# Cross attention with value rows per head and 64x64 products instead of context products

## The reference

```
x = layernorm(x + ttt_attention(x))          # chunked linear attention, 16 heads of 16
x = layernorm(x + cross_attention(x, ctx))   # this part changes
x = layernorm(x + ffn_int8_like(x))          # w_gate_up (1408, 256), w_down (256, 704)

# cross_attention: 16 heads of 128
q = rmsnorm(x @ Wq) * gq;  k = rmsnorm(ctx @ Wk) * gk;  v = ctx @ Wv
P = softmax(q k^T / sqrt(128))               # per batch and head, 64 x 64
out = concat_heads(P v) @ Wo                 # (16, 64, 256)
```

## Time and profile before

| | us |
|---|---|
| median of 3 runs | 442.09 (441.3 to 442.74) |
| the profiled execution | 441.95 |
| its span | 440.1 |
| PE busy | 362.4 (82%) |
| PEld busy | 212.4 (48%) |
| DVE busy | 266.0 (60%) |
| ACT busy | 218.0 (50%) |
| POOL busy | 120.9 (27%) |

### The profile page before, as it was taken

The page is one execution under the profiler, slowest core; times in us unless marked ns, Lnnn a source line. Parts: engine busy times, 40 slices in busy tenths (PEclk is TensorE's granted clock), DMA queues, the critical chain, the costliest instruction groups (busy, mean ns, idle before and its releaser), DMA issues.

```text
span 440.1 us, 10666 instructions
## 1 busy us (share of the span) xinstructions
PE 362.4 (82%) x4506; PEld 212.4 (48%) x4506; DVE 266.0 (60%) x494; ACT 218.0 (50%) x584; POOL 120.9 (27%) x132
## 2 busy tenths in 40 slices
PE   3999979779977735596799999999999999996942
PEld 2445844435433212343465665755757557473621
DVE  1579945499996886504243384673946728367564
ACT  3035954545533333063646757468475584753320
POOL 3042891022040041103033332343223432233001
PEclk9999969988968969589899999999999999998975
DMA  8990000000323001901010010100100100000000
GB/s 260 240 365 11 1 4 5 3 4 3 81 75 101 2 0 35 211 7 48 0 41 11 1 48 12 44 6 13 49 12 25 25 14 0 12 3 0 12 0 25
DMA packets 17630, 19.93 MB, mean 45 GB/s; under 512 B 3360, under 2 KB 15024, under 8 KB 17328
## 3 DMA queue, kind: packets, MB, share of 16 engines
q1 hardware_dynamic: 17552, 19.24, 16.0%
q10 hardware_dynamic: 32, 0.02, 0.0%
HBM read 18.07 MB, written 1.18 MB: 44 GB/s over the span
## 4 chain that ended last, share of the span: by engine, by line
PE 50%; DVE 19%; ACT 13%; POOL 8%; issue 7%; DMA 1%; SPq 1%; POOLq 0%; DVEq 0%; ACTq 0%
PE ps L626 9%; PE ps L535 7%; PE ps L672 5%; PE ps L446 5%; PE ps L525 4%; PE ps L680 3%; PE ps L640 3%; PE ps L572 3%; POOL pr L1525 3%; POOL pr L1527 3%; PE ps L554 3%; PE ps L649 2%; DVE pr L1382 2%; DVE pr L1379 2%; DVE mx L1381 2%
## 5 line engine op out<-in xcount | busy, mean ns | idle before, releaser
L626 PE MATMUL ps<-xwq,x1t 128*128 128x512 f32 x128 | 65.0, 638 | 0.9 <-ACT x1t L997 0.9
L680 PE MATMUL ps<-mvo,cxp 128*128 128x256 f32 x256 | 58.4, 382 | 0.1
L680 PEld LDWEIGHTS ps<-mvo,cxp 128*128 128x128 f32 x256 | 47.6, 190 | 6.7 <-issue 0.4
L535 PE MATMUL ps<-ctxt,xwk 128*128 128x512 f32 x64 | 39.0, 716 | 2.4 <-issue 2.2
L975 ACT ACTIVATE qjunk<-ps 128x128 f32<-128x128 f32 x128 | 33.5, 280 | 9.9 <-PE ps L626 9.7
L896 ACT ACTIVATE ksq<-ps 128x512 f32<-128x512 f32 x32 | 19.0, 594 | 38.3 <-PE ps L525 28.2
L626 PEld LDWEIGHTS ps<-xwq,x1t 128*128 128x128 f32 x128 | 24.0, 202 | 27.5 <-issue 24.7
L985 ACT ACTIVATE qt<-ps 128x512 f32<-128x512 f32 x32 | 19.2, 601 | 23.4 <-PE ps L640 23.3
L525 PE MATMUL ps<-ksq,onehot 128*32 128x512 f32 x64 | 21.8, 680 | 9.2 <-ACT ksq L896 9.1
L672 PE MATMUL ps<-pt,ctx 64*128 64x512 f32 x64 | 28.0, 657 | 0.2 <-ACT cxp L1006 0.2
L975 ACT ACTIVATION_READ_ACCUMULATOR qjunk<-ps 128x1 f32 x128 | 27.1, 212 | 0.0
(11 more groups left out here) (212 smaller groups left out, 736.5 us busy)
## 6 DMA issues: line engine op xcount, KB each, us to landing
rkb<-kscale SPq DMA_DIRECT2D x16, 256.0 KB, 4.0
xn<-in_x_dram SPq DMA_DIRECT2D x4, 512.0 KB, 5.4
ctx<-in_ctx_dram SPq DMA_DIRECT2D x4, 512.0 KB, 8.7
xwo<-in_L_xattn_Wo_dram SPq DMA_DIRECT2D x1, 2048.0 KB, 14.2
xwq<-in_L_xattn_Wq_dram SPq DMA_DIRECT2D x4, 512.0 KB, 5.4
w1n<-in_L_ffn_w_gate_up_dram SPq DMA_DIRECT2D x1, 1408.0 KB, 8.9
xwv<-in_L_xattn_Wv_dram SPq DMA_DIRECT2D x1, 1024.0 KB, 11.0
xwk<-in_L_xattn_Wk_dram SPq DMA_DIRECT2D x1, 1024.0 KB, 16.5
```

The costliest lines, as they stand in the source:

```text
L535: mm(bank(6 + n % 2), xwk[:, h * XD:(h + 1) * XD], ctxt[:, half * BANK:(half + 1) * BANK], start=True, stop=True)\
L626: last = mm(bank(n % 2), x1t[:, (i % 2) * D + k * P:(i % 2) * D + (k + 1) * P], xwq[qn][:, k * BANK:(k + 1) * BANK], start=k == 0, stop=k ...
L680: last = mm(bank(6 + turn_of[("y", i, 0)] % 2, D), cxp[:, h * P:(h + 1) * P], mvo[:, h * D:(h + 1) * D], start=h == 0, stop=h == XH - 1)
```

## The change

The context products and their tile `cxp` go. `value_rows` computes, per tile, ctx (128 rows, both batches) times `mvo` in 8 products of 512 columns, with the same stationary operand (`ctxt`, the transposed context that the keys use); ACT copies them into two tiles `z0` and `z1`, which lie over the context and over Wk of the cross attention. `attention_out` then multiplies, per head and batch, a 64 x 64 block of transposed P by 64 rows of these, 256 columns. The two batches of a head use the upper and the lower 64 partitions of both SBUF and PSUM. `p_transpose` becomes 32 products of 64 x 64 blocks with the identity, so that batch 0 comes out in the upper and batch 1 in the lower half. The value rows of tile 0 are computed in iterations -1 and 0, those of tile i-1 (i from 2) in iteration i. The second load of the context goes. `krow1` moves to another place, and ACT waits for its DMAs before it writes there. `sg` and `gs` of the FFN become one tile.

```diff
+        vrows = [place("z0", XH * D // 2, over="ctx2"), place("z1", XH * D // 2, over="xwk")]
...
+        krow1 = place("krow1", BANK, over="qjunk")
...
-            for half in range(2):
-                load(ctx2[half * T:(half + 1) * T, :].rearrange("p (b c) -> p b c", c=CD), ctx_in.rearrange("b s c -> s b c"), "ctx")
...
                 for n in range(2):
                     bk = open_tp("pt", i, n)
-                    for t in range(4):
-                        col = (i % 2) * XH * T + (n * 4 + t) * P
-                        last = nc.tensor.transpose(bank(bk, P, t * P), pr[:, col:col + P], ident[:, :])
+                    for t in range(8):
+                        for b2 in range(2):
+                            part = slice(b2 * T, (b2 + 1) * T)
+                            col = (i % 2) * XH * T + (n * 8 + t) * T
+                            last = mm(ps[part, bk * BANK + t * T:bk * BANK + (t + 1) * T], pr[part, col:col + T], ident[part, part],
+                                      start=True, stop=True)
...
+            def value_rows(i, n):
+                bk = open_turn("z", i, n)
+                turn_done(mm(bank(bk), ctxt[:, i * P:(i + 1) * P], mvo[:, n * BANK:(n + 1) * BANK], start=True, stop=True))
...
             def attention_out(i, heads):
                 for h in heads:
                     if h == 0:
-                        wait(turn_emptied("cp", i, 3))
+                        pe.wait_ge(sem("tp_evac"), tp_of[("pt", i, 1)] + 1)
+                        wait(turn_emptied("z", i, 3))
                         open_turn("y", i)
-                    last = mm(bank(6 + turn_of[("y", i, 0)] % 2, D), cxp[:, h * P:(h + 1) * P], mvo[:, h * D:(h + 1) * D],
-                              start=h == 0, stop=h == XH - 1)
+                    if h == XH // 2:
+                        wait(turn_emptied("z", i, 7))
+                    at = (6 + turn_of[("y", i, 0)] % 2) * BANK
+                    for b2 in range(2):
+                        part = slice(b2 * T, (b2 + 1) * T)
+                        zh = vrows[h // 8][part, (h % 8) * D:(h % 8 + 1) * D]
+                        last = mm(ps[part, at:at + D], pt[part, h * T:(h + 1) * T], zh, start=h == 0, stop=h == XH - 1)
...
+                if n == 0:
+                    act.wait_ge(sem("k_rows_out"), 64)
...
+            def value_rows_out(i, n):
+                bk = turn("z", i, n)
                 if n == 0 and i >= 1:
                     act.wait_ge(sem("turn_done"), turn_of[("y", i - 1, 0)] + 1)
-                o = cxp[:, :].rearrange("p (h r q) -> p r h q", r=2, q=P)[:, odd, :, b2 * T:(b2 + 1) * T]
-                freed(A(o, bank(bk).rearrange("p (h q) -> p h q", q=T), ACT.Copy))
+                freed(A(vrows[n // 4][:, (n % 4) * BANK:(n % 4 + 1) * BANK], bank(bk), ACT.Copy))
```

More of the change, by code:

```diff
@@ L127, in decoder_block @@
         ctxt = place("ctxt", B * T)
-        krow1 = place("krow1", BANK, over="ctxt")
         pR = place("pR", NCH * CW)
@@ L192, in decoder_block @@
         qjunk = place("qjunk", BANK)
+        krow1 = place("krow1", BANK, over="qjunk")
         assert cursor[0] <= at_of["xwk"]
-        cxp = place("cxp", XH * P)
-        gs = place("gs", FF)
-        assert cursor[0] <= at_of["pR"]
+        vrows = [place("z0", XH * D // 2, over="ctx2"), place("z1", XH * D // 2, over="xwk")]
         xwq = []
@@ L204, in decoder_block @@
         cursor[0] = at_of["sgR"] + KT * BANK
-        sg = place("sg", FF)
+        gs = place("gs", FF)
         hq = place("hq", FF // 2, BF16)
@@ L292, in decoder_block @@
         for i, cur, prev, last2, last3, nxt, nxt2 in pipeline():
+            later = i - 1 if i >= 2 and prev else None
+            first = 0 if i == 0 else None
+            if later is not None:
+                turns += [("z", later, 0, "act"), ("z", later, 1, "act")]
             turns += [("down", i - 3, 0, "dve")] * last3
-            turns += [("cp", i - 1, n, "act") for n in range(2)] * prev
+            if first is not None:
+                turns += [("z", 0, 4, "act"), ("z", 0, 5, "act")]
+            if later is not None:
+                turns += [("z", later, 2, "act"), ("z", later, 3, "act")]
             turns += [("wo", i + 2, 0, "dve")] * nxt2
-            turns += [("cp", i - 1, n, "act") for n in range(2, 4)] * prev
-            turns += [("gu", i - 2, n, "dve") for n in range(4)] * last2
+            if i == -1:
+                turns += [("z", 0, n, "act") for n in range(4)]
+            if first is not None:
+                turns += [("z", 0, 6, "act"), ("z", 0, 7, "act")]
+            if later is not None:
+                turns += [("z", later, 4, "act"), ("z", later, 5, "act")]
+            turns += [("gu", i - 2, n, "dve") for n in range(2)] * last2
+            if later is not None:
+                turns += [("z", later, 6, "act")]
+            turns += [("gu", i - 2, n, "dve") for n in range(2, 4)] * last2
+            if later is not None:
+                turns += [("z", later, 7, "act")]
             turns += [("y", i - 1, 0, "dve")] * prev
@@ L738, in _ @@
             for i, cur, prev, last2, last3, nxt, nxt2 in pipeline():
+                later = i >= 2 and prev
                 if cur:
                     q_quarter(i, 0)
+                if later:
+                    value_rows(i - 1, 0)
                 if last3:
@@ L744, in _ @@
                     q_quarter(i, 1)
+                if later:
+                    value_rows(i - 1, 1)
                 if prev:
@@ L748, in _ @@
                     ffn_down(i - 3)
+                if i == 0:
+                    value_rows(0, 4)
                 if cur:
@@ L751, in _ @@
                     q_transpose(i, 0)
-                if prev:
-                    context_sum(i - 1, 0)
-                    context_sum(i - 1, 1)
+                if i == 0:
+                    value_rows(0, 5)
+                if later:
+                    value_rows(i - 1, 2)
                 if cur:
                     q_quarter(i, 3)
+                if later:
+                    value_rows(i - 1, 3)
+                if cur:
                     q_transpose(i, 1)
@@ L759, in _ @@
                     ttt_out(i + 2)
-                if prev:
-                    context_sum(i - 1, 2)
+                if i == -1:
+                    for n in range(4):
+                        value_rows(0, n)
+                if i == 0:
+                    value_rows(0, 6)
+                if later:
+                    value_rows(i - 1, 4)
                 if cur:
                     q_transpose(i, 2)
+                if i == 0:
+                    value_rows(0, 7)
                 if last2:
                     x_transpose_q(i - 2)
-                if prev:
-                    context_sum(i - 1, 3)
+                if later:
+                    value_rows(i - 1, 5)
                 if last2:
                     gate_up(i - 2, range(0, 2))
+                if later:
+                    value_rows(i - 1, 6)
                 if cur:
@@ L773, in _ @@
                     gate_up(i - 2, range(2, 4))
+                if later:
+                    value_rows(i - 1, 7)
                 if cur:
@@ L1015, in silus @@
                     act.wait_ge(*turn_emptied("gu", i, 2 * n))
-                    A(sg[:, n * FP:(n + 1) * FP], gs[:, n * FP:(n + 1) * FP], ACT.Silu, scale=sx[:, 8 * (i % 3):8 * (i % 3) + 1])\
+                    A(gs[:, n * FP:(n + 1) * FP], gs[:, n * FP:(n + 1) * FP], ACT.Silu, scale=sx[:, 8 * (i % 3):8 * (i % 3) + 1])\
                         .then_inc(sem("sg_ready"), 1)
             for i, cur, prev, last2, last3, nxt, nxt2 in pipeline():
+                later = i >= 2 and prev
                 if cur:
                     q_quarter(i, 0)
+                if later:
+                    value_rows_out(i - 1, 0)
                 if last3:
@@ L1025, in _ @@
                     q_quarter(i, 1)
+                if later:
+                    value_rows_out(i - 1, 1)
                 if prev:
@@ L1028, in _ @@
                     tp_out("pt", i - 1, 1)
+                if i == 0:
+                    value_rows_out(0, 4)
                 if cur:
@@ L1031, in _ @@
                     q_quarter(i, 2)
-                if prev:
-                    context_out(i - 1, 0)
-                    context_out(i - 1, 1)
+                if i == 0:
+                    value_rows_out(0, 5)
+                if later:
+                    value_rows_out(i - 1, 2)
+                    value_rows_out(i - 1, 3)
                 if cur:
@@ L1037, in _ @@
                     q_quarter(i, 3)
-                if prev:
-                    context_out(i - 1, 2)
+                if i == -1:
+                    for n in range(4):
+                        value_rows_out(0, n)
+                if i == 0:
+                    value_rows_out(0, 6)
+                if later:
+                    value_rows_out(i - 1, 4)
                 if cur:
                     tp_out("qt", i, 2)
```

(11 more changed lines are left out.)

3 lines of the change are left out of this document (removed).

## The result

| | us |
|---|---|
| before, in the same comparison | 442.41 median of 4 (441.3 to 452.76) |
| after | 479.1 median of 4 (475.81 to 490.69) |
| ratio | 1.081, 95% interval 1.071 to 1.092 |
| predicted | 471.8 (465 to 485) |

The ratio and the medians of 477.16 (after) and 442.09 (before, +35.1) leave out the slowest execution of each kernel, and for the changed kernel that one, 490.69 us with a span of 488.3, is the profiled one. Its pipeline begins at 193.37 us where the one of before begins at 178.80. So I compare the pipeline alone, from the first `ttt_out` to the end of the span: 261.3 us before, 488.3 - 193.37 = 294.9 after, +33.6. That is nearly all of the 35.1.

A forecast was written before the change was run, and what follows sets the result against it. PE's own work was taken to set the period, so PE slots were counted: +4.8 us per tile before idle. Summed by iteration this gave +29.8 on 441.95, 471.8 us, range 465 to 479, upper end 485 with the first two rivals.

The forecast's parts named there:

- iteration 1: No value rows or context products: -3.2, P transposes +1.5 at low clock, wait on ACT +0.9, together -0.8 us.
- attention_out unchanged in slots: Per tile, 64 instructions whose two batches run at once take 32 slots of 0.22, 7.0 us again: +0.
- P transposes +1.1: p_transpose per tile: 64 small instructions take 2.0 us instead of 0.93 for 8; bounds +0 to +2.9.
- Value rows 6.86: Added products on PE: 16 instructions of 0.429 us, 6.86 us per tile; bounds 6.8 to 7.4.
- The idle that the change fills: Iterations 3 to 5: z0 and z1 before p_transpose fill its 0.84 us of idle, leaving +4.0 each.
- a bound of 1.3: ACT's queue: up to 1.3 us per iteration if a value row's copy always stands ahead of the wanted one.
- a rival at 483: attention_out's 64-row tile is slower, 1.03 ns a column: +1.4 x 8 = 11, 483 us; chance 0.10.
- The start: Before x1_transpose: z0 to z3 delay it by 5.3 us, less if the clock returns earlier; middle taken, +2.4.
- My low end: Start, if the clock returns early: value rows cost 3.4, query products give back up to 3, -0.6 net; x1_transpose from 183.4.
- Iteration 8: z0 and z1 lie in the 3.04 us idle before P; then 10.0 against 9.77, +0.5 with one ACT wait.
- the one that halves attention_out: All four instructions of a head run at once, 3.5 us less a tile: 443.8 us, or 440.8; chance 0.03.
- The rival of the clock: Half-used tiles count as idleness; clock falls to 1.2 GHz in half of each attention_out: +28, 500 us; chance 0.03.

The follow-up runs named there:

- experiment 2: Changed kernel with the value rows of tile 0 only, those of tiles 1 to 7 left out: 443.23 us, period 26.65, pipeline 259.5.
- Experiment 1: Changed kernel with attention_out's products reordered, eight heads of batch 0, then eight of batch 1: 526.3 us, period 38.16, pipeline 334.6.
- experiment 3: Changed kernel with P transposed whole, eight transposes of 128x128, blocks left in the wrong places: 471.41 us, period 31.63, pipeline 286.1.
- experiment 7: Changed kernel with the value rows z6 ahead of gate/up: periods 32.37 (iterations 3 to 5) and 32.20 (6 and 7), pipeline 291.3 us.
- Experiments 4: Kernel before, probabilities copied batch by batch so the context products read contiguous columns: ratio 1.0003 (0.9951 to 1.0055), pipeline 261.1 us.
- experiment 6: Changed kernel with x1_transpose behind both halves of attention_out and value rows z0 ahead of query quarter 0: period 33.17, pipeline 295.9 us.
- experiment 5: Kernel before with the third and fourth context product issued twice in a row: period 29.60 us, a group 1.91 us against 1.05.
- experiment 8: Changed kernel with odd heads of attention_out on the other two array quarters, their sums not added: 460.99 us, period 30.39, pipeline 279.2.

## Why the prediction was right, and where it was short

The direction and its reason were right: PE's slots add up, and the value rows are what costs (experiment 2). By the steps, in us of the pipeline:

| step | predicted | measured |
|---|---|---|
| start and iteration 0 | +4.9 | +2.7 |
| iteration 1 | -0.8 | -1.3 |
| iteration 2 | +4.8 | +6.1 |
| iterations 3 to 5, each | +4.0 | +5.0 |
| iteration 6 | +4.0 | +5.5 |
| iteration 7 | +4.4 | +5.9 |
| iteration 8 up to attention_out | +0.5 | 0.0 |
| attention_out of tile 7 and behind | 0 | -0.4 |
| sum | +29.8 | +33.6 |

- **attention_out unchanged in slots: right.** 7.20 us against 7.02, because the two batches overlap. Experiment 1 is the proof; it puts a price of 5.3 us a period on the loss of the overlap. The Trainium skill, "TensorEngine Tiling (Array Packing)", says in its Gotcha 1: PSUM Pressure that different row tiles cannot access the same PSUM bank simultaneously. The traces do not agree for tiles that write different partitions of one bank: attention_out does it with two at once at the full rate, 216 ns for a pair, and the earlier trace rows with 3.6. Two row tiles writing the same partitions of one bank were not tried.
- **P transposes +1.1: right** (2.01 against 0.93; experiment 3).
- **Value rows 6.86: too low by 0.6, and past my bound of 7.4.** Summed over an iteration they take 7.48 us less idle. Four take 0.86; z1 and z7, ahead of a product of another tiling, and z5 and z6, ahead of and behind a stop at gate/up, take 0.95 to 1.08.
- **The idle that the change fills: too high.** I let 0.84 us of P's wait vanish and kept 0.3. P's wait did vanish, but PE is idle 0.66 us a period after (1.13 before) and 1.6 in iterations 6 and 7. Of these, 0.32 and 1.2 are for ACT's copy of xqt, which stands behind copies of value rows; 0.19 are for a bank that DVE empties. I had the copies as a bound of 1.3 and took nothing more than the 0.3 of before. By order alone experiment 7 shortens these periods by 0.5 and 0.75 us.
- **The array's tiling: missed.** The context rows showed 0.53 us per instruction, and I read them as a possible slow tile, a rival at 483. Experiments 4 and 5 show neither access nor tile but the change between tilings, 0.05 to 0.1 us on each side (a first slot of 267 instead of 216 ns in attention_out, on the side of P 107 instead of 59). x1_transpose between the halves therefore takes 0.37 instead of 0.22, and attention_out 0.18 more: +0.33 a period, which experiment 6 mostly takes away. The Trainium skill, "TensorEngine Tiling (Array Packing)", says in its Key Properties that changing the tiling mode drains the engine. The runs agree in that every change costs, with 0.05 to 0.1 us as the price of one side. But there are no more such changes than before (11 a period after, 12 before), and I also missed what the context products had cost their neighbours.
- **The account of one period.** Iteration 4 by line, after less before, idle apart: value rows +7.48, context products -3.17, P +1.09, attention_out +0.19, x1_transpose +0.15, gate/up +0.21; `ttt_out` and the transposes that stood beside context products -0.34; the query products -0.16, since the last one ahead of P's wait had taken 592 instead of 429 ns; idle -0.45. Together +5.0, against a forecast of +4.0.
- **The start: too dear, through the clock.** The four value rows delay x1_transpose from 5.19 to 8.42 us behind the first product, +3.2 of at most 5.3. But PE had no gap there (8.28 of 8.42 us busy), and the clock was back on 1.00 from the query products on, where it had been 0.64 before:

```profile
193.37:201.79 8.42, 8.28 (x16) 4.30 (x17) 3.45 (x9) 1.79 (x3) 1.57 (x4) 0.66 0.32 72
201.79:216.84 15.05, 13.57 (x47) 7.05 (x45) 1.03 (x3) 11.34 (x46) 1.87 (x2) 1.00 0.02 3
```

In the third row, 12 instructions of the query products took 8.11 us (clock 0.64 from 185.16 to 193.27); after, eight of them take 3.54:

```profile
202.92 3.70 PE L639 MATMUL ps<-xwq,x1t 128*128 128x512 f32 x8 [0.74 <-ACT x1t L1035]
206.46 1.02 PE L681 MATMUL ps<-mvo,ctxt 128*128 128x512 f32 x2
```

How much too dear is open. The stretch up to the first scores took 20.77 us in the trace that I worked from, but 19.43 in experiment 5, whose code is the same there, at a mean clock of 0.77 instead of 0.71. Against that the changed kernel's 23.47 would be +4.0. My low end was wrong as well: value rows that cost 3.4 and query products that give back 3 are +0.4 net, not -0.6, and x1_transpose could not come before 182.4 + 3.4 = 185.8, let alone at 183.4. It came at 187.2, counted from the same start.

- **Iteration 8: right in kind.** z0 and z1 lie in the wait for P, of which 0.58 us are left.
- **The sum: nearer than its terms.** Iterations 2 to 7 came out some 7.4 us dearer than forecast. The start, iterations 1 and 8 and the end came out some 3.6 cheaper, so half of the miss does not show in the total. The forecast's own upper end was also added up short: 471.8 + 2.9 + 1.5 + 4 is 480, not 479.

Of the rivals, the one that halves attention_out is real as a mechanism (experiment 8) but not in this kernel, where only the two quarters on the diagonal are used; with it the period falls by 2.5 us, and the result would still be slower. The rival of the clock is out: it stands at 1.00 in iterations 2 to 7. Why the stage ahead of the pipeline took up to 14.6 us more in some profiled executions was not studied.

## What to carry to other kernels

When products are reordered, count the columns that TensorE streams one after the other, not the multiplications. (ctx M) costs 4096 columns a tile at full height. (P ctx) costs 2048 at half height, and two halves can run at once; in the kernel before only one pair of the four did, which leaves 1536. attention_out needs half the multiplications after, but its 4096 columns stayed, and it saved no time. Over both products the multiplications grow by 20% (84 to 101 million a tile, an estimate from the shapes), the columns by 45% (5632 to 8192), and the time by 44% (10.2 to 14.7 us). Put small products on different row and column parts next to each other, and group those of one tiling, since every change of tiling is paid on both sides. Where PE sets the period, a wait costs more than the idle that the profile shows, as the slots around it are longer too.

## What the runs showed of the hardware

- 64x64 products on the two quarters of the diagonal overlap fully, into one bank: start to start 216 ns for a pair of 256 float32 columns (profile of after); on all four quarters (two banks) 216 ns for four (experiment 8); on the same quarter 216 ns for one (experiment 1).
- A 64-row tile runs at the full rate, 0.43 us for 512 float32 columns, contiguous or in 8 pieces of 64 (experiments 4 and 5). A change of tiling costs 0.05 to 0.1 us in the first slot behind it and 0.09 in the last ahead of it. The first slot after a wait is as long: 533 instead of 429 ns for 512 columns, 164 instead of 108 for 128.
